# One attention-plus-experts layer on one core: score products one unit further ahead, logits in quarter tiles, two TensorE updates per expert chunk

## The reference

```python
# attention, 16 heads of 8, windows of 64 tokens every 32 tokens (7 per sequence; the last one counts twice)
scores = einsum(qw, kw) * scale + pos_bias
ow     = softmax(scores) @ vw            # added up over the overlapping windows, divided by the counts
x      = layernorm(x + (merged @ Wo + bo))
# eight experts, the best two of each token
logits = x @ router_w.T;  g = sigmoid(top2(logits)), normalised
out    = sum_e g_e * (silu(x @ w_gate[e]) * (x @ w_up[e])) @ w_down[e]
x      = layernorm(x + out)
```

## Time and profile before

| | |
|---|---|
| median of three runs | 895.55 us (891.91 to 898.95) |
| the profiled execution | 893.16 us, of which the span is 891.4 us |
| busy: PE, DVE, POOL, ACT | 712.7, 510.3, 429.9, 365.9 us |
| mean granted clock | 0.935 |

### The profile page before, as it was taken

How to read it: one execution, slowest core, us unless ns; L and a number is a source line. 1 busy time by engine, 2 the same in 40 slices (tenths; PEclk the granted TensorE clock), 3 DMA queues, 4 the chain that set the end, 5 groups by cost and what they waited for, 6 DMA issues and landing times. The chain is left out here.

```text
span 891.4 us, 33669 instructions
## 1 busy us (share of the span) xinstructions
PE 712.7 (80%) x13562; PEld 574.6 (64%) x13562; DVE 510.3 (57%) x1623; ACT 365.9 (41%) x546; POOL 429.9 (48%) x483
## 2 busy tenths in 40 slices
PE   5599999999899898899899998777678787787600
PEld 2376766776676776766676776677667677777500
DVE  7545665665665666666666674355543444454357
ACT  3144334334334334334334332444434455455338
POOL 8422155355355354354355443655555655555545
PEclk8899999999999999999999998788998999999955
DMA  6873443443543443544543401232223322222177
GB/s 164 246 221 93 117 124 118 125 123 116 126 124 113 129 124 113 129 125 110 132 124 114 117 22 31 74 106 60 66 77 100 95 73 73 72 74 81 42 294 280
DMA packets 84025, 103.56 MB, mean 116 GB/s; under 512 B 15936, under 2 KB 70592, under 8 KB 83872
## 3 DMA queue, kind: packets, MB, share of 16 engines
q1 hardware_dynamic: 75232, 83.57, 32.5%
q0 software_dynamic: 8640, 17.84, 6.3%
HBM read 60.12 MB, written 40.79 MB: 113 GB/s over the span
## 5 line engine op out<-in xcount | busy, mean ns | idle before, releaser
L760 DVE TENSOR_REDUCE neg_max<-score_ps 128x16 f32<-128x1024 f32 x109 | 133.4, 1223 | 142.6 <-PE score_ps L1166 139.9
L281 POOL DMA_INDIRECT slots<-rows_sb,slot_at x128 | 127.1, 993 | 159.3 <-PE o_ps L1219 133.0
L537 POOL DMA_INDIRECT results<-scaled_sb,result_at x142 | 136.2, 959 | 114.5 <-DVE scaled_sb L1029 78.5
L672 ACT ACTIVATE prob<-scoret_ps 128x1024 f32<-128x1024 f32 x112 | 114.6, 1023 | 180.6 <-PE scoret_ps L1166 177.3
L1219 PE MATMUL o_ps<-v_sb,prob 128*32 128x18 f32 x7168 | 93.2, 187 | 13.4 <-issue 13.1
L1219 PEld LDWEIGHTS o_ps<-v_sb,prob 128*32 128x32 f32 x7168 | 78.3, 110 | 26.9 <-issue 19.2
L1203 PE MATMUL scoret_ps<-max_rows,half 128*64 128x512 bf16 x448 | 69.5, 388 | 26.3 <-DMA max_rows<-maxt_sb 26.3
L705 ACT CAST w_slot<-wgu_sb 128x1024 fp32r x71 | 74.9, 1055 | 0.4 <-issue 0.3
L1166 PE MATMUL scoret_ps<-blocks,stack 128*64 128x256 f16 x920 | 71.6, 277 | 0.0
L1186 PE MATMUL scoret_ps<-bias_hl,fold 128*64 128x512 f16 x448 | 70.1, 393 | 1.7 <-issue 1.0
L1166 PE MATMUL score_ps<-blocks,stack 128*64 128x256 f16 x872 | 67.0, 274 | 2.7 <-DMA blocks<-scratch 2.7
(11 more groups left out here) (177 smaller groups left out, 1565.4 us busy)
## 6 DMA issues: line engine op xcount, KB each, us to landing
scratch<-qk_hl SPq DMA_DIRECT2D x128, 128.0 KB
stack<-scratch SPq DMA_DIRECT2D x32, 512.0 KB
blocks<-scratch SPq DMA_DIRECT2D x128, 128.0 KB
xin<-slots SPq DMA_DIRECT2D x71, 130.0 KB
blocks<-results SPq DMA_DIRECT2D x16, 512.0 KB, 6.3
x_sb<-in_x SPq DMA_DIRECT2D x16, 256.0 KB
out<-y_sb SPq DMA_DIRECT2D x16, 256.0 KB, 3.9
results<-scaled_sb,result_at POOLq DMA_INDIRECT x142
```

Source lines behind the costliest of these rows:

```text
L281: nc.gpsimd.indirect_dma_start(slots, bass.IndirectOffsetOnAxis(ap=slot_at[:, k % 2, n:n + 1], axis=0), rows_sb[:, k % 2, n // TT, n % TT, ...
L537: pool.indirect_dma_start(results, bass.IndirectOffsetOnAxis(ap=result_at[s % RBUF][:, t:t + 1], axis=0), scaled_sb[:, s % RBUF, t, :], No ...
L672: act.activation(prob[:, (par + u) % 2, :], scoret_ps[:, :, :].rearrange("p b c -> p (b c)"), ACT.Exp).then_inc(exp_done, 1)
L760: dve.tensor_reduce(neg_max[:, par, v, :], ps[:, :, :].rearrange("p b (h k) -> p (b h) k", k=W), AX_X, ALU.max, negate=True).then_inc(max_ ...
```

## The change

There are four parts. The products for the maxima run one unit further ahead from step 1 on: turn u makes unit u+1 of step i+1, the maxima are turned and copied at turn 6 instead of 7, and turn 8 also makes unit 0 of step i+2, on PE and on DVE. The logits are made in 16 products of 32 columns of weights each, instead of four of 128. In the last step POOL makes the fill first, and the power in front of scatters 4 to 7. In the expert stage PE updates `up_ps` and `y_ps` only (and `xt2_ps` for the first three chunks): `silu(s)` waits for the up half, and `high(s)` for `down(s - 3)`, which follows the transposes in PE's order.

```diff
@@ POOL, step
                 def step(i, par, first, last):
+                    if last:
+                        make_fill()
                     if not first:
                         deviation(i - 1)
...
-                    if last:
-                        scatter(i - 2, 4)
-                        scatter(i - 2, 5)
-                        make_fill()
                     if not first:
                         powers(i - 1)
...
                     if last:
-                        scatter(i - 2, 6)
-                        scatter(i - 2, 7)
+                        for n in range(TT, TOP * TT):
+                            scatter(i - 2, n)
                         routed(i - 1)
@@ ACT
                 def high(s):
-                    act.wait_ge(xt2_ps, s + 1)
+                    if s < 3:
+                        act.wait_ge(xt2_ps, s + 1)
+                    else:
+                        act.wait_ge(y_ps, s - 2)
...
                 def silu(s):
-                    act.wait_ge(gate_ps, s + 1)
+                    act.wait_ge(up_ps, s + 1)
@@ DVE, step
                         if there(i + 1):
-                            if u < NU:
-                                maximum(i + 1, 1 - par, u)
-                            if u == NU:
+                            v = u if first else u + 1
+                            if v < NU:
+                                maximum(i + 1, 1 - par, v)
+                            if u == (NU if first else NU - 1):
                                 max_copy(i + 1)
...
+                        if u == NU + 1 and there(i + 2):
+                            maximum(i + 2, par, 0)
@@ PE, logits
                     for t in range(TT):
-                        last = pe.matmul(bank[1 if there(k + 1) else 0][:, t * E:(t + 1) * E], x1t_sb[:, t * P:(t + 1) * P], rw_sb[:, :],
-                                         start=True, stop=True)
+                        for quarter in range(4):
+                            rows = slice(32 * quarter, 32 * quarter + 32)
+                            last = pe.matmul(bank[1 if there(k + 1) else 0][rows, t * E:(t + 1) * E],
+                                             x1t_sb[:, t * P + 32 * quarter:t * P + 32 * quarter + 32], rw_sb[:, :],
+                                             start=True, stop=True)
@@ PE, step
-                            if there(i + 1):
-                                if u or first:
-                                    bias_s(i + 1, u)
-                                scores(i + 1, 1 - par, u)
+                            v = u if first else u + 1
+                            if there(i + 1) and v < NU:
+                                bias_s(i + 1, v)
+                                scores(i + 1, 1 - par, v)
+                        if u == (NU if first else NU - 1) and there(i + 1):
+                            turn_maxima(i + 1, 1 - par)
...
                         if u == NU and there(i + 1):
-                            turn_maxima(i + 1, 1 - par)
                             project_v(i + 1, 1 - par, 1)
                         if u == NU + 1:
...
                             if there(i + 2):
                                 bias_s(i + 2, 0)
+                                scores(i + 2, par, 0)
@@ PE, turn and gate_up
-                    last.then_inc(xt2_ps, 1)
+                    if s < 3:
+                        last.then_inc(xt2_ps, 1)
...
-                    for n, signal in ((0, gate_ps), (1, up_ps)):
+                    for n in range(2):
                         for hh in range(2):
...
-                        last.then_inc(signal, 1)
+                    last.then_inc(up_ps, 1)
```

More of the change, by code:

```diff
@@ L242, in build @@
         fill_made, tables_begun = sem("fill_made"), sem("tables_begun")
-        gate_ps, up_ps, silu_done, h_done = sem("gate_ps"), sem("up_ps"), sem("silu_done"), sem("h_done")
+        up_ps, silu_done, h_done = sem("up_ps"), sem("silu_done"), sem("h_done")
         y_ps, scaled, result_out = sem("y_ps"), sem("scaled"), [sem(f"result_out{n}") for n in range(RBUF)]
```

## The result

| | median, us | profiled execution's span, us | mean granted clock |
|---|---|---|---|
| before (20 runs) | 895.5 (889.99 to 903.32) | 891.4 | 0.935 |
| after (20 runs) | 904.99 (896.49 to 913.03) | 909.3 | 0.921 |

The ratio of after to before is 1.0089, 95% interval 1.0067 to 1.0111: 0.9% slower, some 8 us, where 5% faster was forecast.

The account below looks back on a forecast made before the run. PE's order of work bounds attention; in the expert stage no engine is full and PE's updates arrive late. 893.16 - 19 - 9.8 - 2 - 14 = 848.4 us, with the median 2.4 us higher: forecast 850 us, range 820 to 877.

Parts of the forecast that it names:

- part 4: Expert stage: two PE updates a chunk instead of four, forecast to win 14 us.
- outside a hold both added waits are covered: Expert stage: silu's added 0.71 us and the copy's 1.15 us cost nothing unless PE's updates arrive 1 to 3.5 us late.
- the value taken for a hold: Expert stage: 0.6 us won each time PE's updates come late after POOL starts indirect transfers, 23.7 times, 14 us.
- the rival of the two waits in series: Expert stage: late updates delay silu 0.71 us and the copy 1.15 us more, 44 us lost, 908 us; chance 0.07.
- The rival of holds that shrink with the number of updates: Expert stage: each late update costs its own turn, so fewer updates also remove long waits, 825 us; chance 0.17.
- Part 1: Attention: products one unit ahead remove most of PE's 28.1 us of waits at step borders, saving 19 us (10 to 28).
- it adds no product: Attention: working one unit ahead only moves a pair of blocks from each turn to the turn before.
- The read-back at turn 8: Attention: operands for the added product arrive 2.7 us early, costing nothing; the rival that they are late, 869 us, had 0.08.
- Part 2: Attention: quarter tiles cut a block of logits from 0.99 to 0.34 us in 15 steps, saving 9.8 us.
- all of it PE time on the path: Attention: the 9.8 us saved in the logits' blocks shorten the kernel in full.
- Part 3: Last step: POOL's new order ends DVE's 1.92 us wait for the power, saving 2 us (0 to 4).
- Both ways in which the text said that it would be wrong: Waits of the same size come up at DVE's `gates`, or the expert stage moves by more than 30 us.

Follow-up runs that it names:

- a3_updates: Kernel before with only two PE updates a chunk in the expert stage and both waits (silu's, the copy's) moved: 913.46 us, ratio 1.0147.
- b4_ahead_quarter: Kernel before with products one unit further ahead and quarter-tile logits, nothing else: 893.88 us, ratio 0.9947.
- b2_high_on_y: Kernel before with the turned rows' copy waiting for the down products, their own update only for three chunks: 909.23 us, ratio 1.0112.
- b3_waits_only: Kernel before with both expert-stage waits moved as in the change, but all four updates still made: 906.05 us, ratio 1.0091.
- a1_ahead: Kernel before with only the products for the maxima one unit further ahead: 894.64 us, ratio 0.9927.
- a2_quarter: Kernel before with only the logits in quarter tiles: 899.22 us, ratio 0.9978.
- d2_aq_values64: Kernel before with products one unit ahead, quarter-tile logits and value products in 64-column tiles; expert stage and last step unchanged: 871.82 us, ratio 0.9740.
- d3_after_copy: Changed kernel with the turned rows' copy waiting for their own update again, made in every chunk: 898.54 us, ratio 1.0059 to the kernel before.
- e2_pool64: d2_aq_values64 plus the change's POOL order in the last step, on another chip: 784.59 us, ratio 0.9721 to the kernel before.

## Why the prediction was wrong

**The sign failed in part 4**, at the sentence that outside a hold both added waits are covered, and at the value taken for a hold. 14 us won were forecast; a3_updates lost 13 (1.0147), and the changed kernel against b4_ahead_quarter loses 1.0089 / 0.9947, also 13. What the runs showed in the place of the step: on the kernel before, the copy isn't covered (b2_high_on_y, 1.0112). It was the one piece of ACT's work that could be done early, and `down` stands 1.34 us behind it with the weights and `x_lo` queued behind (b2_high_on_y, 43.7 us of waits). The measured end lies below nothing, where the rival of the two waits in series stood. That rival named the place rightly (the copy, the weights and the next silu behind y) and the price wrongly: 44 us, where it was 12 to 14. Its other half, silu, costs 1.0025 alone, within no change. In the changed kernel itself the shares are others: with the copy's wait put back it is still at 1.0059, so most of the 13 us lies there with silu's wait and POOL's order together, and which of the two isn't settled. The rival was given 0.07, since one ACT row seemed to show an update coming through during a hold. A single row was weak ground for 14 us.

The premise that fewer updates help fell with b3_waits_only: two updates more cost nothing. The rival of holds that shrink with the number of updates fell with it. Whether updates queue in a hold no run shows. The value for a hold was also counted for the whole stage (71 / 3) though its pattern had been seen in the second half alone.

**Part 1 was right in its mechanism and too large.** Both waits went, and the waits that remain or come instead are 0.59 us a step (8.3 us in a1_ahead) where the arithmetic of the step had 0.65. That they agree is partly luck: 0.5 us is left of the old waits and 7.8 us stands in front of `bias_s`, 0.56 us a step, for which only 0.1 was allowed. The step that failed is "it adds no product", from which I took the value products as they were. They lost 8.6 us more, 5.1 of them at the borders of the program's blocks. Gained: 0.7%, 6.5 us of 19. Between the first and the last `project_out`, PE's idle time fell from 44.8 to 37.5 us, 7.3 us, which fits. The read-back at turn 8 held: no wait of `score_ps` for `blocks` stands in after's list.

**Part 2 was right for the block and wrong for the path.** 0.39 us a block against 0.34, so weight loads of this form do overlap with the products. The Trainium skill's rule that they overlap only where they go to other rows ("TensorE: Matmul & The Clock Gate", Part 3, The mechanism) isn't borne out by this case. The failing words are "all of it PE time on the path". At these places PE didn't wait for its array; it waited for its program, and 48 more instructions a block had to come in the time that the shorter block saved (a2_quarter 0.9978). In a2_quarter the stops at the borders of the program's blocks are 8.3 us where they were 1.2. d2_aq_values64 shows the 9 us once instructions are fewer. The step behind it: I priced a block by the fastest of its kind. From first to last record a value block of the kernel before takes 0.56 us in the median and 0.78 in the mean, so more than a quarter of the sum was something other than the block at its best. That fewer us of array work can need more instructions per us wasn't asked. The 8.6 us of "issue" that the kernel before shows there would not have told by themselves: only 1.2 of them are at a border.

**Part 3** did what it says: in after DVE doesn't wait for the power any more, 1.92 us in the earlier trace rows:

```profile
565.08 0.16 DVE L839 TENSOR_SCALAR expo<-expo 128x8 f32<-128x8 f32 x1
```

Alone it gave nothing that the interval of 3 us either way can tell (1.0000), within the bounds given. Whether the scatters it postpones take the 2 us back wasn't tried.

**The sum**: 895.5 - 6.5 - 2 + 0 + 13 = 900 us from the parts alone, and 905 was measured. The 5 us left, 0.5%, are of the size of the intervals; the miss of d3_after_copy says that silu's wait or POOL's order costs more beside the others than alone.

**The points named to watch**: L1254 gone, L1203 under 0.5 us, logits at 0.34: these hold within 0.05 us. From one turn of the maxima to the next it is 33.5 us before and 33.8 after (medians), not 2 less. The expert stage took 286 and not 258 us, 12.1 us for three chunks in the mean where the kernel before takes 11.5; the forecast of 9.4 was set against a group of three of 10.0. Both ways in which the text said that it would be wrong were the wrong ones to name.

## What to carry over

When a kernel's busiest engine stops without a semaphore inside a long row of small instructions, see how many instructions it needs per us, and whether its stops stand at a fixed place in its program, before shortening its array time. Here half the instructions for the same products made the value block 0.3 us longer, took all stops at the borders of the program's blocks away, and turned a saving in the logits that was worth nothing into 9 us. Price a block by the mean over all of its kind, and say what that mean holds: stops inside it, or waits behind it.

Before letting a cheap step wait for a later event of the same engine, list what is in order behind the waiter; a row in which it happened to be late already isn't cover.

The best kernel was the change's two attention parts with value products of 64 columns, and the expert stage as before: 0.974, 871.8 us for 893.65. On the last chip e2_pool64, with POOL's new order on top, gave 0.9721, 784.6 us for 808.05.

## What was not expected of the hardware

- PE can lack instructions. In rows of 32-column products, at 64 records in 0.67 us, fourteen stops of up to 3.8 us (15.4 us in after) begin at one place of a block of 256 of PE's records and end 1.2 to 1.6 us behind a packet of 16 KB of the queue "instruction". With 32 records in 0.99 us these stops are gone. The transfers of the read-back (76.8% of the engines) seem to hold the packet up; that is argued from one stretch and wasn't tried.
- A stop of 3.78 us cost more than itself: the three blocks behind it ran at a granted clock of 0.50, at 0.86 us instead of 0.46.
- The holds depend on the chip or its state, and not on the kernel alone. In the traces of the four other batches, on three chips, the expert stage lasts 271 to 287 us and is full of them; on the last chip it lasts 185 to 189 us, with the same POOL instructions at the same spacing. So a row of indirect transfers isn't enough to make a hold. What makes one stays open. No part of the change was measured by itself on that chip.
